# A two-phase hybrid block on one Trainium2 core: the passage from the state-space phase to the attention phase reordered

## What is computed

```python
x = x + attn_a(layernorm(x))      # Mamba mixer, scan over 512 tokens, feed-forward
x = x + ffn(layernorm(x))         # recurrence over the batches
x = x + attn_b(layernorm(x))      # 16 heads of width 16, full softmax over 512 tokens
x = x + ffn(layernorm(x))

def attn_b(x):
    xw  = einsum('bhtd,hde->bhte', x_h, w_att_val)
    att = softmax(einsum('bhte,bhse->bhts', xw, x_h) / sqrt(16))
    v   = x @ wv_w.T + wv_b
    return einsum('bhts,bhsd->bhtd', att, v_heads) @ out_w.T + out_b

def ffn(x):                       # c: the state, one row per token, starts at in_c
    step: f, i = sigmoid(...), sigmoid(...); g = tanh(...); c = f * c + i * g
    return tanh(x @ wo.T + c_final @ uo.T + bo)
```

## Time and profile before

| | us |
|---|---|
| median of 3 runs | 1522.29 |
| runs | 1521.08, 1522.29, 1682.96 |
| the profiled execution | 1525.04 |
| its span, first to last instruction | 1523.3 |

### The profile page before, as it was taken

How to read it: one execution, slowest core, us unless ns; L and a number is a source line. 1 busy time by engine, 2 the same in 40 slices (tenths; PEclk the granted TensorE clock), 3 DMA queues, 4 the chain that set the end, 5 groups by cost and what they waited for, 6 DMA issues and landing times.

```text
span 1523.3 us, 17326 instructions
## 1 busy us (share of the span) xinstructions
PE 1365.3 (90%) x5574; PEld 664.6 (44%) x5574; DVE 1129.6 (74%) x1814; ACT 857.9 (56%) x1488; POOL 646.1 (42%) x387
## 2 busy tenths in 40 slices
PE   6427799999999998999858889999999999999998
PEld 2103445454545555555422334444445454444444
DVE  4889888989899898931278877786868777776335
ACT  6656676767676764531104656556565656555633
POOL 2596969797969685723033212213130222100000
PEclk9757999999999999999957999999999999999999
DMA  4843443434343433012073333343232433330145
GB/s 139 285 143 112 127 151 130 139 134 138 137 137 96 160 139 112 28 42 69 25 168 85 91 79 78 78 98 85 59 96 59 98 72 68 72 71 3 35 143 170
DMA packets 93802, 158.04 MB, mean 104 GB/s; under 512 B 8608, under 2 KB 74720, under 8 KB 90592
## 3 DMA queue, kind: packets, MB, share of 16 engines
q1 hardware_dynamic: 93712, 156.94, 35.7%
HBM read 110.91 MB, written 46.01 MB: 103 GB/s over the span
## 4 chain that ended last, share of the span: by engine, by line
PE 61%; DVE 15%; issue 10%; POOL 6%; ACT 5%; DMA 2%; SPq 0%; POOLq 0%; ACTq 0%; DVEq 0%
PE psum L1070 23%; PE psum L2055 8%; PE psum L1989 7%; PE psum L1963 6%; PE psum L1978 5%; DVE mx L1452 5%; PE psum L1933 4%; DVE psum L566 3%; PE psum L1122 2%; POOL hb L1003 2%; PE psum L1095 1%; DVE middle L549 1%; DVE stats L1428 1%; ACT back L796 1%; PE psum L2150 1%
## 5 line engine op out<-in xcount | busy, mean ns | idle before, releaser
L1703 ACT ACTIVATE pw<-psum 128x512 f32<-128x512 f32 x512 | 302.1, 598 | 274.3 <-PE psum L1978 270.9
L1452 DVE TENSOR_REDUCE mx<-psum 128x1 f32<-128x512 f32 x512 | 344.0, 686 | 151.7 <-PE psum L1963 150.5
L1003 POOL TENSOR_TENSOR hb<-ddb,bcb 128x1024 f32<-128x1024 f32 x127 | 296.6, 2359 | 69.0 <-DVE middle L549 54.5
L566 DVE TENSOR_TENSOR_SCAN psum<-psum,hb 128x512 f32<-128x512 f32 x224 | 261.6, 1213 | 22.9 <-POOL hb L1003 12.2
L1963 PE MATMUL psum<-kp,qp 96*128 96x512 bf16 x512 | 203.6, 403 | 33.0 <-DVE mx L1452 21.6
L792 ACT ACTIVATE psum<-ddb,A_neg 128x512 f32<-128x512 f32 x256 | 165.4, 682 | 84.0 <-DVE hb L569 67.1
L1978 PE MATMUL psum<-qp,kp 99*128 99x512 bf16 x512 | 197.6, 387 | 5.0 <-ACT pw L1703 4.3
L1871 POOL TENSOR_TENSOR rstd<-rstd,neg_half 128x4 f32<-128x4 f32 x16 | 16.3, 1017 | 415.2 <-DVE rstd L1437 415.2
L569 DVE TENSOR_TENSOR hb<-psum,bcb 128x1024 f32<-128x1024 f32 x112 | 137.2, 1225 | 3.9
L1989 PE MATMUL psum<-pw,v_sb 128*32 128x512 f32 x1024 | 124.3, 602 | 0.5 <-ACT pw L1703 0.5
L1070 PE MATMUL psum<-back,w 128*128 128x512 f32 x256 | 114.9, 600 | 4.0 <-ACT back L808 1.9
(11 more groups left out here) (214 smaller groups left out, 2085.2 us busy)
## 6 DMA issues: line engine op xcount, KB each, us to landing
ddb<-dd SPq DMA_DIRECT2D x64, 512.0 KB, 6.8
bcb<-bc SPq DMA_DIRECT2D x32, 512.0 KB, 6.7
parts<-parts_sb SPq DMA_DIRECT2D x96, 128.0 KB
qp<-parts SPq DMA_DIRECT2D x32, 256.0 KB, 7.8
dd<-dd_out SPq DMA_DIRECT2D x7, 1024.0 KB, 4.9
kp<-parts SPq DMA_DIRECT2D x16, 384.0 KB, 4.7
x_back<-x_dram SPq DMA_DIRECT2D x9, 512.0 KB, 8.4
xh_back<-xh SPq DMA_DIRECT2D x8, 512.0 KB, 3.8
```

The lines of the kernel that those rows point to most:

```text
L566: e.tensor_tensor_scan(to[:, g, :], a[:, g, :], h[:, g, :], 0.0, ALU.mult, ALU.add).then_inc(scan_ok, 1)
L1003: e.tensor_tensor(hb[n % NHB], ddb[k % NSLOT][:, 1:2, :].to_broadcast([P, 2, L]), bcb[q][:, 0, :, :], ALU.mult).then_inc(bx_ok, 2 if n == ...
L1452: used.up(e.tensor_reduce(mx[u % 2][:, n:n + 1], score_bank(used.n), AXIS.X, ALU.max))
L1703: e.activation(pw[n % NPW], bank(5 + n % 2), ACT.Exp, scale=HD ** -0.5).then_inc(exp_ok, 1)
```

## The change

Four edits, all between the phases:

1. **First unit in two halves of heads.** `first_fetch` replaces the fetch of unit 0: heads 0 to 3 of k and then of q (seven transfers, counted on a new semaphore `qk_first`), then heads 4 to 7 of both (seven, counted on `qk_in[0]`). The parts of unit 1 are sent behind these. Score 0 of unit 0 waits for `qk_first`, score 16 for `qk_in[0]`.
2. **Norm of batch 1 on ScalarE.** `second_power` on GpSimd computes the power and the product of negative mean and rstd. `second_apply` on ScalarE applies them with four ACTIVATEs (Identity with scale and bias) at s = 0 and 1 of p = -1. VectorE's `front_apply` is left out for batch 1. The statistics of batch 2 wait until ScalarE has read those of batch 1.
3. **New state on ScalarE.** `restart` becomes two ACTIVATEs (Identity, scale 0, bias twice in_c) at s = 19 of p = -4; GpSimd's `restart` is gone.
4. **First maxima's parts.** For unit 0 both `minus_part` follow directly on `minus` at s = 17.

```diff
             def send(b, n, c):
+                if b == 2:
+                    e.wait_ge(qk_first, 112)
...
+            def rows_in(u, n, heads, done):
+                b, f, s = u // 2, u % 2, u % 3
+                name, dst = ("k", kp[s]) if n else ("q", qp[s])
+                r = 0
+                for cs in QK_ROWS[name]:
+                    block = slice(r, r + len(cs) * HD)
+                    src = part_dram[b % 2][n, f, cs[0]:cs[-1] + 1].rearrange("c e h t -> (c e) h t")
+                    e.dma_start(dst[block, heads, :], src[:, heads, :]).then_inc(done, 16)
+                    r = block.stop
...
+            def first_fetch():
+                for n in (1, 0):
+                    e.wait_ge(part_sent[2 * n], 48)
+                    rows_in(0, n, slice(0, HU // 2), qk_first)
+                for n in (1, 0):
+                    rows_in(0, n, slice(HU // 2, HU), qk_in[0])
...
-            for f in range(NF):
-                first_send(f)
-                fetch(f)
+            first_send(0)
+            first_fetch()
+            first_send(1)
+            fetch(1)
...
-                    if s in (0, 1) and odd and front:
+                    if s in (0, 1) and odd and front and b + 2 != 1:
                         front_apply(b + 2, s)
...
+                    if s == 17 and p == -1:
+                        minus_part(0, 1)
+                        minus_part(0, 2)
-                    if s in (18, 19) and 0 <= p + 1 < NU:
+                    if s in (18, 19) and 0 < p + 1 < NU:
                         minus_part(p + 1, s - 17)
...
                     if s == 28 and not odd and front:
+                        if b + 2 == 2:
+                            e.wait_ge(xa_ok, 4)
                         spread_end(0, a_var)
...
+            def restart():
+                e.wait_ge(cuo_pe, 2)
+                for f in range(NF):
+                    e.activation(c_state[:, f, :], ident[:, 0:1].to_broadcast([P, L]), ACT.Identity, bias=in_c2[:, f:f + 1],
+                                 scale=0.0).then_inc(c2_init, 1)
+
+            def second_apply(k):
+                e.wait_ge(a_rstd, 2)
+                for t in (2 * k, 2 * k + 1):
+                    ins = e.activation(tok(A0)[:, t, :], x2[1][:, t, :], ACT.Identity, bias=f_nb[:, 0, t:t + 1], scale=rstd[0][:, t:t + 1])
+                ins.then_inc(xa_ok, 1)
...
                     if s == 19 and p == -4:
                         first_tanh()
+                        restart()
+                    if s in (0, 1) and p == -1:
+                        second_apply(s)
...
-            def restart():
-                e.memset(c_state, 0.0).then_inc(c2_init, 1)
-                for f in range(NF):
-                    e.wait_ge(c2_init, 1)
-                    e.tensor_scalar(c_state[:, f, :], c_state[:, f, :], in_c2[:, f:f + 1], None, ALU.add).then_inc(c2_init, 1)
...
+            def second_power():
+                e.wait_ge(a_var, 2)
+                own.up(e.tensor_scalar(f_neg.unsqueeze(2), mv[0][:, :, 0:1], -1.0, None, ALU.mult))
+                own.up(e.tensor_tensor(rstd[0], rstd[0], neg_half[:, 0:NT], ALU.pow))
+                e.wait_ge(own.sem, own.n)
+                e.tensor_tensor(f_nb[:, 0, :], f_neg, rstd[0], ALU.mult).then_inc(a_rstd, 1)
...
-                    power(0, a_var, b + 3, a_rstd)
+                    if b + 2 == 1:
+                        second_power()
+                    else:
+                        power(0, a_var, b + 3, a_rstd)
...
-                if n == 0:
+                if n == 0 and u == 0:
+                    e.wait_ge(qk_first, 112)
+                if n == (NSC // 2 if u == 0 else 0):
                     e.wait_ge(qk_in[u % 3], 112 * (u // 3 + 1))
```

More of the change, by code:

```diff
@@ L1343, in first_send @@
                         e.dma_start(part_dram[0][n, f, c].rearrange("e h t -> h e t"), parts[n][:, c, f]).then_inc(part_sent[2 * n], 16)
+            def rows_in(u, n, heads, done):
[7 more added lines that the diff above has]
+                    r = block.stop
             def fetch(u):
-                b, f, s = u // 2, u % 2, u % 3
                 if u >= 3:
                     e.wait_ge(st_pe, NSC * (u - 2))
-                for n, name, dst in ((1, "k", kp[s]), (0, "q", qp[s])):
-                    e.wait_ge(part_sent[2 * n + b % 2], 48 if u == 0 else 96 * (b // 2 + 1))
-                    r = 0
-                    for cs in QK_ROWS[name]:
-                        block = slice(r, r + len(cs) * HD)
-                        e.dma_start(dst[block], part_dram[b % 2][n, f, cs[0]:cs[-1] + 1].rearrange("c e h t -> (c e) h t")
-                                    ).then_inc(qk_in[s], 16)
-                        r = block.stop
+                for n in (1, 0):
+                    e.wait_ge(part_sent[2 * n + u // 2 % 2], 96 * (u // 4 + 1))
+                    rows_in(u, n, slice(0, HU), qk_in[u % 3])
+            def first_fetch():
+                for n in (1, 0):
+                    e.wait_ge(part_sent[2 * n], 48)
+                    rows_in(0, n, slice(0, HU // 2), qk_first)
+                for n in (1, 0):
+                    rows_in(0, n, slice(HU // 2, HU), qk_in[0])
             def xwo_store(b):
@@ L1579, in gate_keep @@
                 if b == 0:
-                    e.wait_ge(c2_init, 1 + NF)
+                    e.wait_ge(c2_init, NF)
                 else:
```

3 lines of the change are left out of this document (1 added, 2 removed).

## The result

| | before | after |
|---|---|---|
| median, us | 1522.29 | 1515.74 |
| runs, us | 1521.1 to 1526.7, one of 1683.0 | 1515.2 to 1517.5 (5 runs) |
| profiled execution, us | 1525.04 | 1515.18 |
| its span, us | 1523.3 | 1513.4 |

The ratio of the times is 0.9949, 7.8 us, with a 95% interval of 0.9933 to 0.9964: 5.5 to 10.2 us faster. The difference of the medians is 6.55 us; the forecast was 5.4. The execution of 1683.0 us is a slow one and is not in the ratio.

The account below looks back on a forecast made before the run. Bound by the bytes of unit 0's fetch before the first score, then by VectorE's maxima up to the first exponential. 4.0 + 1.9 - 0.5 = 5.4 us, so 1522.3 becomes 1516.9 us; range 1513.4 to 1520.8.

Parts of the forecast that it names:

- Halves: Unit 0's k and q fetch: fewer bytes in front of the first score make it earlier, gain 4.0 us (0 to 5.4).
- 393 thousand bytes at 131 GB/s take 3.0 us: First half of unit 0's q rows: moving from 774.7 us, through at 777.7, landed at 778.9.
- what is queued behind took no share: Unit 0's fetch, 776 to 782 us: unit 1's parts, issued behind the q rows from 775.28, took no DMA bandwidth.
- The thin cover of unit 1's fetch: Unit 1's q rows land near 797.5 us, TensorE wants them at 799: cover 3.3 us, cost nothing.
- a transfer's time goes by its rows: Rival for unit 0's fetch: half the bytes land no sooner, at 782.9; kernel slower, about 1524 us; chance 0.08.
- Norm: Batch 1's norm: VectorE loses four instructions before the first exponential, gain 1.9 us (0 to 2.0).
- State: New state moved from GpSimd to ScalarE: nothing on the path; up to 2.4 us before the first turned tile if late.
- Stretch: Unit 0's maxima parts run without maxima between them; no maximum fills GpSimd's hold of VectorE, loss 0.5 us (0 to 2.1).
- From there the same distance to the end, 703.5 us: Sign in the changed profile: from the first exponential's matmul, near 814.4 us, to the end the length stays 703.5 us.
- a shift at 819.83 should reach the end of the kernel: First exponential's matmul: TensorE is nearly full afterwards and everything hangs by data, so an earlier start carries through whole.
- the shift is given back: Rival: later clock rise or worse GpSimd collisions in following units take 3 to 4 us of 5.4; about 1520.5 us, chance 0.14.
- the case of more: Rival: first half at 777.5 us, no collision, clock up earlier; gain 8.4 us, 1513.9 us, chance 0.13.

Follow-up runs that it names:

- before with unit 2's stretch: The kernel before, with both `minus_part` of unit 2 directly on `minus` at s = 17; median 1521.26 us, ratio 0.9986 (0.9972 to 1.0000).

## Why the prediction was right

The measured median of 1515.74 lies in the range, 1.2 us from 1516.9. The two edits that were to pay did pay where they act, by the mechanisms named. That the number came so close is in part luck. From batch 0's norm to the first exponential the profiles differ by 7.3 us and not 5.4, and behind it by another 1.7, where nothing was forecast; but the profiled execution of before lay 2.75 us above its median and that of after 0.56 below, and that takes 3.3 us back. How much of the pieces is the change and how much is those two executions, one trace of each can't tell.

- **Halves: 4.0 predicted, 5.74 in the profile** (5.1 against the shortest D1 with whole rows). The mechanism was right, fewer bytes in front of the first score, and the size was off, near or beyond its upper bound of 5.4. The step that failed is "393 thousand bytes at 131 GB/s take 3.0 us": I gave the first piece the rate of the tail of 1.57 MB of whole rows. The DMA engines moved 211 to 215 GB/s and the 14 transfers landed after 2.1 to 3.5 us. With half rows that were all awaited together they moved 167 GB/s from 776 to 782 us. So the length of the pieces is some of it, 0.7 to 1.3 us for all 1.57 MB, but not all of it: whole k rows had moved at 253. How the rest divides no run shows. The first piece of two heads left pieces of 6 KB for the rest, and all rows then took 12.2 us from the first issue to the last landing, against 10.3 in the changed kernel.
- **Two readings of the DMA rows were off.** The share from 776 to 782 was 0.86 and not full, and "what is queued behind took no share" does not fit the bytes: from 772 to 783 us all traffic was 1.90 MB and the rows are 1.57. What the parts behind cost the first score was 0.6 us at most.
- **The thin cover of unit 1's fetch.** Predicted to land 1.5 to 2.5 us later; its q rows were issued 2.4 us sooner (1.5 measured from batch 0's norm), because the parts of unit 1 were through 1.7 us sooner, although they were issued 3.1 us later. The rival that a transfer's time goes by its rows falls: with as many rows and half of the bytes the first seven transfers took 2.1 to 3.3 us instead of 5.1 to 8.1. The advice of the Trainium skill (DMA: Bandwidth & Descriptors, Rules for kernel authors) to coalesce transfers speaks against this change; here the transfers of 64 to 192 KB landed sooner than those of 128 to 384 KB, and the measurement decides.
- **Norm: 1.9 predicted.** Alone it made D2 1.45 shorter, and the transposes came 1.9 sooner behind the first score. The normed batch came 13.4 us behind the first maximum (13.7 predicted), the transposes 14.3 behind it (14.3 predicted), with cover left. That it costs 0.9 us in unit 5 was not foreseen.
- **State: nothing predicted, 0.6 alone.** The failed step was to count GpSimd's adds as beside the path. They slowed VectorE's norm from 0.40 to 0.55 us for each instruction on the mean. In the changed kernel this and the norm are nearly the same gain: behind the first score the transposes come 1.90 us sooner with the norm alone, 0.60 with the state alone and 2.10 with all edits. (In D2 the single differences happen to add up, -1.45 - 0.60 + 0.49 = -1.56 against -1.59, but D2 scatters by 0.5.)
- **Stretch: 0.5 of loss predicted, 0.49 and 0.52 measured in D2**, by the profile once added and once taken away, and nearly all of it behind `minus`.
- **"From there the same distance to the end, 703.5 us": wrong by 1.66 us.** It was 701.81, and in the experiments 700.59 to 705.81. The step that failed is "a shift at 819.83 should reach the end of the kernel". The units from 2 on take the same time but for unit 5, but units 0 and 1 don't: they contain the collisions with GpSimd and the stretches at half clock. With the halves alone this piece gives back 1.3 us, with the state alone 0.8 and with the norm alone 2.3. With all edits it adds 1.7. I had this as a rival ("the shift is given back", 0.14) and set the clock at 0 plus or minus 1.5, and both were too little: unit 1 alone varies from 34.3 to 38.4 us.
- **The range.** Its lower end, 1513.4, is called the case of more, but that case gives 1513.9. The result lies above both.

Why the whole is more than its parts: the ratios of the four single edits add up to 0.2% slower, together they are 0.5% faster. What is shown is that in unit 1 VectorE is held by GpSimd when it comes 0.14 us late and not when it comes 0.37 us early, and that taking this hold away from the kernel with the halves shortens the unit by 4.0 us, of which 1.5 come back in unit 2. The Trainium skill (SBUF — State Buffer, SBUF: two separate sides) says that an instruction keeps the shared port pair for its whole length; the trace agrees in unit 1, 2.12 us of VectorE beside 2.12 of GpSimd. In unit 5 of before it was GpSimd's instruction that waited, by 0.6 us, the length of VectorE's, although its row starts 0.08 us ahead; so the starts of two rows don't tell within a tenth of a microsecond which of them was first.

What is not shown is that the four edits make the kernel escape. In its trace TensorE is already at half clock in the first hold, the exponentials behind it come later, with them ScalarE's cast and GpSimd's difference. The traces of the other kernels go by this clock too, and one kernel without the four edits, before with unit 2's stretch, has GpSimd's difference as late. So an escape may be the more frequent case with the change, or belong to the execution that was profiled; the one trace of each kernel can't decide it, and I could not set the clock in an experiment. The change did not aim at it. That part of the gain is open, and it may not survive the next edit: with a first piece of two heads the hold was back.

## What to carry to other kernels

A transfer that everything waits for is worth cutting where its first part is enough to start, and the rate of the pieces has to be measured and not taken from the whole. Where two engines that hold each other run close together, a shift of some tenths of a microsecond upstream can switch a hold of 2 us on or off far behind; count such places in the trace before adding up a sum. Judge an edit by the pieces of the span, for a single edit's time can have the other sign than its local gain, but first look whether the two traces agree up to the place of the edit: where they don't, the difference behind it is not yet the edit's. Freeing an engine that is the bound also frees what the moved work collided with, so two edits can share one gain.

## What the runs showed of the hardware

- 96 rows of k and 96 of q, read from DRAM in pieces of 4 KB by transfers of 64 to 192 KB, landed 2.1 to 3.8 us after issue, and after 3.4 to 5.0 in the kernel whose first score awaits all of unit 0; in pieces of 8 KB, with twice the bytes a transfer, after 4.4 to 8.4 us, and pieces of 6 KB took up to 5.1. All 1.57 MB of a unit took 10.0 to 10.8 us from the first issue to the last landing in 4 KB pieces and 10.9 to 12.1 in 8 KB pieces; with nothing queued behind them it was 11.4. Which part of the path makes them slower no run shows.
- From unit 2 on, units took the same time in different kernels to within 0.05 us, with two exceptions: 0.9 us in unit 5, in all six kernels with batch 1's norm on ScalarE, and 1.5 us in unit 2 beside a half-clock stretch.
- GpSimd's difference of q came 5.40 to 5.54 us behind `minus` in the five traces in which TensorE's granted clock had fallen to half (1.2 GHz) there, and 3.93 or 3.94 us in the nine in which it was full.
